# Top-k by a threshold and a counted mask in a windowed attention kernel

## What is computed

```python
k_windows = q_h[:, idx, :]                       # the 64 tokens up to this one
diff = k_windows - q_h[:, :, None, :]
dist = jnp.sqrt((diff * diff * m_h).sum(axis=-1) + 1e-08)
dist = jnp.where(mask[None], dist, jnp.inf)
neg_d, loc = jax.lax.top_k(-dist, K)             # K = 32 of 64
infl = jnp.exp(neg_d)
infl = infl / (infl.sum(axis=-1, keepdims=True) + 1e-08)
context = jnp.einsum('btk,btkd->btd', infl, neighbor_v)
```

## Time and profile before

| | |
|---|---|
| median of 3 runs | 865.25 us (864.89 to 867.82) |
| the profiled execution | 865.7 us |
| its span, first to last instruction | 863.9 us |
| mean granted TensorE clock | 0.895 of full speed |
| busy: DVE | 795.0 us, 92% of the span |
| busy: PE (matmuls) | 764.0 us, 88% |
| busy: ACT | 620.0 us, 72% |
| busy: POOL | 461.4 us, 53% |
| DMA | 27.27 MB in 49233 packets |

### The profile page before, as it was taken

One profiled execution on the slowest core, in us unless ns is written; L12 is line 12 of the kernel. 1 busy time (PEld: TensorE's weight loads), 2 busy tenths in 40 slices (PEclk: granted clock), 3 DMA queues, 4 the chain that ended last, 5 costly groups with the idle time before them and its releaser, 6 DMA issues.

```text
span 863.9 us, 21621 instructions
## 1 busy us (share of the span) xinstructions
PE 764.0 (88%) x4885; PEld 500.8 (58%) x4885; DVE 795.0 (92%) x6746; ACT 620.0 (72%) x1862; POOL 461.4 (53%) x870
## 2 busy tenths in 40 slices
PE   5987999998899999888989988999889898989975
PEld 3444556565566665556666655666556666655644
DVE  5865999799999998999999999979999999999890
ACT  3982466687777876777877787668777777877763
POOL 1113455565556665556666665556555565666442
PEclk9995777799999987999999999779999999998775
DMA  5300000010000000011001110001010100110000
GB/s 164 106 21 16 23 18 25 21 30 28 29 29 29 26 27 27 29 30 30 25 28 30 31 30 28 28 21 31 27 30 29 30 30 23 31 31 29 23 9 10
DMA packets 49233, 27.27 MB, mean 32 GB/s; under 512 B 5513, under 2 KB 48593, under 8 KB 49105
## 3 DMA queue, kind: packets, MB, share of 16 engines
q1 hardware_dynamic: 49104, 25.90, 10.1%
HBM read 10.28 MB, written 4.19 MB: 17 GB/s over the span
## 4 chain that ended last, share of the span: by engine, by line
DVE 75%; PE 17%; ACT 3%; issue 2%; DMA 2%; POOL 1%; SPq 0%; POOLq 0%; ACTq 0%
DVE work L939 39%; DVE m L929 26%; DVE key L955 4%; PE psC L1167 2%; PE psD L1112 2%; PE psW L1183 2%; PE psD L1012 2%; PE psD L1104 1%; DVE den L972 1%; DMA big<-in_x 1%; PE psW L1185 1%; PE psW L1194 1%; PE psW L1136 1%; PE psX L1119 1%; PE psC L1095 1%
## 5 line engine op out<-in xcount | busy, mean ns | idle before, releaser
L939 DVE MATCH_REPLACE8 work<-m,work 128x64 f32<-128x64 f32 x1536 | 300.6, 204 | 0.0
L929 DVE MAX8 m<-work 128x8 f32<-128x64 f32 x1536 | 210.2, 205 | 0.0
L471 POOL TENSOR_TENSOR big<-work,con 128x512 f32<-128x512 f32 x128 | 161.7, 1286 | 21.5 <-ACT work L617 21.5
L1167 PE MATMUL psC<-vst,big 128*128 128x34 f32 x1024 | 139.6, 282 | 0.0
L1167 PEld LDWEIGHTS psC<-vst,big 128*128 128x128 f32 x1024 | 125.2, 193 | 17.1 <-issue 2.1
L450 POOL TENSOR_TENSOR hsc<-gat,rnn 128x8 f32<-128x8 f32 x64 | 13.0, 204 | 222.4 <-ACT rnn L699 222.4
L1136 PE MATMUL psW<-con,big 128*128 128x128 f32 x512 | 92.2, 309 | 27.8 <-POOL big L471 19.5
L939 DVE MATCH_VALUE_LOAD work<-m,work 128x8 f32 x1536 | 113.0, 74 | 0.0
L1136 PEld LDWEIGHTS psW<-con,big 128*128 128x128 f32 x512 | 62.5, 155 | 64.7 <-POOL big L471 46.7
L939 DVE MATCH_REPLACE8 work<-m,key 128x64 f32<-128x64 f32 x512 | 99.9, 203 | 0.0
L676 ACT ACTIVATE key<-key,bias 128x512 f32<-128x512 f32 x64 | 46.2, 722 | 55.2 <-DVE key L955 55.2
(11 more groups left out here) (204 smaller groups left out, 1630.9 us busy)
## 6 DMA issues: line engine op xcount, KB each, us to landing
hst<-hT_all SPq DMA_DIRECT2D x64, 96.0 KB
tst<-qT_all SPq DMA_DIRECT2D x256, 17.0 KB
big<-in_x SPq DMA_DIRECT2D x16, 256.0 KB, 2.8
xs<-in_x SPq DMA_DIRECT2D x64, 64.0 KB, 1.9
out<-yo SPq DMA_DIRECT2D x64, 64.0 KB, 1.6
sst<-nst SPq DMA_DIRECT2D x128, 3.0 KB
tst<-nst SPq DMA_DIRECT2D x128, 2.0 KB
con<-in_consts SPq DMA_DIRECT2D x1, 549.5 KB, 5.4
```

What stands on the lines that cost most here:

```text
L471: nc.gpsimd.tensor_tensor(wun[:, s, heads].rearrange("p h (v j) -> p h v j", v=2), work[:, s].rearrange("p (h j) -> p h j", h=NH)[:, heads ...
L929: last = v.max(m8[:, h], src[:, h * WIN:(h + 1) * WIN])
L939: last = v.match_replace(work[:, s, cols], m8[:, h], src[:, cols], GONE)
L1167: last = mm(pC[:, h * 2 * VD:(h + 1) * 2 * VD], wts[:, s, h], vst[:, s4, h].rearrange("p v e -> p (v e)"), start=True, stop=True)
```

## The change

It alters what is selected, how, and the order of the queues.
- **Distances.** Each token half (64 rows) gets a matmul of its own with its own 160 columns (64 slots of the block before, 32 columns for query and low-rank product, 64 slots of its own block): 16 distance matmuls of 64 x 160 instead of 8 of 128 x 224. Masks shrink to 160 columns per group. Slot j of the result is a token by its place in the block, so key needs one relu (ACT) and one max/min (DVE).
- **Selection.** It runs on squared distances. Slots j and j+32 are compared: the smaller 32 go to one list, the negated larger 32 to the other. DVE takes the 16 largest of each list with two MAX8 rounds and one match_replace per head and list. The smallest of the 16 maxima of opposite ranks is the threshold theta, the value of the 32nd smallest.
- **Mask.** POOL subtracts theta from key (diff); PE transposes diff to slots in partitions; ACT takes Sign of diff + 1e-30 and of diff - 1e-30 (fst, bf16); two matmuls with count_bf count, so that of equal distances the right number is kept; DVE compares with KEEP and multiplies with the weight (wsel). The weights come from a transpose of key itself on PE (pXT), and Ln, Exp, Exp on ACT (infl).
- **Context.** POOL multiplies wsel by two 0/1 masks, of_own and of_before (wab). The slots already lie in partitions, so 8 matmuls (4 pairs of heads x 2) follow with values vst, which are kept per block of 64 tokens for a whole sequence. The 8 transposes and two copies to wts go, hst and its DMA go.
- **Order.** Output and second layer norm come a step later (chunk i-4). On ACT, infl of chunk i+1 and lnn, rnn stand ahead of yo of chunk i-4. On PE, the transpose of key of chunk i+1 stands behind the distances of chunk i+2. SP waits for yo of chunk i-4, then issues the copies for chunk i+3 as before, without hst. n_c moves from ACT to POOL.
- **Matmuls without a reader.** Three of 320 columns before the wait for wab, three of 256 before the wait for osp; the two of 240 columns ahead of the context and the two groups of 448-column ones go.

The diff, cut to its core:

```diff
-            def step(i, ph):
...
+            def step(i):
+                k = i - 4
+                if there(k):
                     sync.wait_ge(yo_ready, k + 1)
...
-                    sync.dma_start(hst[:, s], hT_all[:, bass.ds(c0, 3 * WIN)]).then_inc(rows_in[s], 16)
...
+                    sync.wait_ge(s_ready, k + 1)
                     for g in range(NG):
-                        sync.dma_start(sst[HD:P:32, s, g, 0:3 * WIN], nst[g:NH:NG, s]).then_inc(rows_in[s], 16)
+                        sync.dma_start(sst[HD:P:32, s, g].rearrange("p (n x) -> p n x", n=3)[:, :, 0:WIN],
+                                       nst[g:NH:NG, s].rearrange("p (n x) -> p n x", n=3)).then_inc(rows_in[s], 16)
...
+                    nc.gpsimd.tensor_tensor(diff.rearrange("p (h j) -> p h j", h=NH),
+                                            key[:, k % 2].rearrange("p (h j) -> p h j", h=NH),
+                                            theta[:, k % 2].unsqueeze(2).broadcast_to([P, NH, WIN]),
...
+                    nc.scalar.activation(fst[:, 0], pDT, ACT.Sign, bias=bias[:, 4:5]).then_inc(f_ready, 1)
+                    nc.scalar.activation(fst[:, 1], pDT, ACT.Sign, bias=bias[:, 5:6]).then_inc(f_ready, 1)
...
+                k = i + 1
+                if there(k):
+                    e = infl[:, k % 2]
...
+                    act.wait_ge(xT_ready, k + 1)
...
+                    nc.scalar.activation(e, pXT, ACT.Ln, bias=bias[:, 1:2]).then_inc(ln_done, 1)
...
+                    nc.scalar.activation(e, e, ACT.Exp, scale=0.5).then_inc(root_done, 1)
...
+                    nc.scalar.activation(e, e, ACT.Exp, scale=-1.0).then_inc(infl_ready, 1)
...
+                    nc.scalar.activation(lnn[:], n2[:, k % 4], ACT.Ln, bias=bias[:, 6:7]).then_inc(lnn_done, 1)
+                    act.wait_ge(lnn_done, k + 1)
+                    nc.scalar.activation(rnn[:, k % 2], lnn[:], ACT.Exp, scale=-0.5).then_inc(rnn_ready, 1)
+
+                k = i - 4
+                if there(k):
+                    act.wait_ge(y_ready, k + 1)
+                    need(act, po_ready, min(k + 3, NCH))
+                    need(act, out_in[k % 2], 16 * (k // 2))
...
+            def pick(rnd, u):
+
+                where = slice(8 * rnd, 8 * rnd + 8)
+                for h in range(NH):
+                    last = v.max(top[:, u, h, where], low_high[:, u, h])
+                last.then_inc(picked, 1)
+
+            def drop(u):
+
+                for h in range(NH):
+                    last = v.match_replace(low_high[:, u, h], top[:, u, h, 0:8], low_high[:, u, h], GONE)
...
+                    v.tensor_tensor(low_high[:, 1], x4[:, :, 0], x4[:, :, 1], ALU.max).then_inc(pair_done, 1)
+                    v.tensor_tensor(low_high[:, 0], x4[:, :, 0], x4[:, :, 1], ALU.min).then_inc(pair_done, 1)
+                    dve.wait_ge(pair_done, 3 * i + 1)
+                    v.tensor_scalar(low_high[:, 1], low_high[:, 1], -1.0, None, ALU.mult).then_inc(pair_done, 1)
...
+                    v.scalar_tensor_tensor(out=wsel, in0=pZ, scalar=KEEP, in1=infl[:, k % 2], op0=ALU.is_ge,
+                                           op1=ALU.mult).then_inc(w_ready, 1)
...
+                    v.scalar_tensor_tensor(out=meet, in0=top[:, 1], scalar=-1.0, in1=top[:, 0], op0=ALU.mult,
+                                           op1=ALU.max).then_inc(meet_done, 1)
+                    dve.wait_ge(meet_done, i + 1)
+                    need(dve, diff_ready, i - 1)
+                    v.tensor_reduce(theta[:, i % 2], meet, AX_X, ALU.min).then_inc(theta_ready, 1)
...
-                        last = mm(bank_of(r)[:, g, 0:SW], tst[strip, s, g], sst[strip, s, g], start=False,
-                                  stop=(g == NG - 1), skip_group_check=True)
+                        for late in range(2):
+                            toks = slice(late * WIN, (late + 1) * WIN)
+                            last = mm(bank_of(r)[toks, g, 0:PW], tst[strip, s, g, toks], sst[strip, s, g, late * B0:late * B0 + PW],
+                                      start=False, stop=(g == NG - 1), skip_group_check=True)
...
+                    keep_clock(psC, PW, 3)
+                    pe.wait_ge(wab_ready, 2 * k + 2)
...
+                        o = pC[:, r * 2 * VP:(r + 1) * 2 * VP].rearrange("p (v x) -> p v x", v=2)
+                        mm(o, wab[:, k % 2, 0, cols], vst[:, blk + 1:blk + 3, r], start=True, stop=False)
+                        last = mm(o, wab[:, k % 2, 1, cols], vst[:, blk:blk + 2, r], start=False, stop=True)
...
+                    mm(pZ, count_bf[:, 0], fst[:, 0], start=True, stop=False)
+                    mm(pZ, count_bf[:, 1], fst[:, 1], start=False, stop=True).then_inc(count_ready, 1)
...
+                k = i + 2
+                if there(k):
+                    pe.wait_ge(rows_in[k % 2], ROWS_IN * (k // 2) + ROWS_IN)
...
+                    distances(k % 2).then_inc(dist_ready, 1)
+
+                k = i + 3
+                if there(k):
...
+                k = i + 1
+                if there(k):
+                    pe.wait_ge(d2_ready, k + 1)
+                    need(pe, vst_ready, 2 * (k - 1))
+                    for r in range(4):
+                        last = nc.tensor.transpose(pXT[:, r * P:(r + 1) * P], key[:, k % 2, r * P:(r + 1) * P], ident)
+                    last.then_inc(xT_ready, 1)
...
+                    keep_clock(psX[:, 2 * P:4 * P], P, 3)
+                    pe.wait_ge(osp_ready, k + 1)
+                    nc.tensor.transpose(pO, osp[:, k % 2], ident).then_inc(po_ready, 1)
...
```

More of the change, by code:

```diff
@@ L54, in constants @@
     before = np.where(j > i, 0.0, BIG)
[L56 to L59, removed]
+    c[:, C_MASK:C_MASK + PW] = np.concatenate([before, np.zeros((P, QW)), own], 1)
+    slot = (np.arange(P) % WIN)[:, None]
+    tok = (np.arange(CH) % WIN)[None, :]
+    c[:, C_OWN:C_OWN + CH] = slot <= tok
+    c[:, C_OWN + CH:C_OWN + 2 * CH] = slot > tok
     e = np.arange(P) % 32
@@ L75, in constants, with counting, adaln_block @@
     return c
-def adaln_block(nc, x, encq, encv, w1, b1, w2, b2, base, hebu, hebv, dec, wr, amat, bmat, cin, wmod, consts, out):
+def counting():
+    jp, j = np.arange(WIN)[:, None], np.arange(WIN)[None, :]
+    eye, after = (jp == j).astype(np.float32), (jp >= j).astype(np.float32)
+    below, equal = 97.0 * eye - 1.0, 33.0 * eye - after
+    m = np.zeros((P, 2, P), np.float32)
+    for a in range(2):
+        rows = slice(a * WIN, (a + 1) * WIN)
+        m[rows, 0, rows] = 0.5 * (equal - below)
+        m[rows, 1, rows] = -0.5 * equal
+    return m
+def adaln_block(nc, x, encq, encv, w1, b1, w2, b2, base, hebu, hebv, dec, wr, amat, bmat, cin, wmod, consts, counts, out):
     ctx = ExitStack()
@@ L149, in adaln_block @@
         bsc = big[:].rearrange("p a s (b d) -> p (a s) b d", b=NB)
-        hst = sb("hst", [P, 2, 3 * WIN])
         tst = sb("tst", [P, 2, NG, CH])
         sst = sb("sst", [P, 2, NG, SW])
[L154 to L160, removed]
+        sqs = sb("sqs", [P, NG, 3 * WIN])
+        nst = sb("nst", [2 * NH, 2, 3 * WIN])
+        selm = sb("selm", [P, NB, NG, 2 * NH])
+        low_high = modn_all[:, 0:NH * WIN].rearrange("p (u h j) -> p u h j", u=2, h=NH)
+        top = gsgn_all[:].rearrange("p u (h n) -> p u h n", h=NH)
+        meet = gabs_all[:, 0].rearrange("p (h n) -> p h n", h=NH)
+        theta = sb("theta", [P, 2, NH])
+        diff = wmod_sb[:, 0:NH * WIN]
+        fst = sb("fst", [P, 2, 4 * CH], BF16)
+        infl = z8_all[:, 0:8 * CH].rearrange("p (s x) -> p s x", s=2)
+        wab = big[:, 0].rearrange("p s (v x) -> p s v x", v=2)
+        wsel = big[:, 1, 0, 0:4 * CH]
+        count_f = big[:, 1, 1, 0:2 * P]
+        vst = sb("vst", [P, NBLK, 4, VP])
         qh = sb("qh", [P, 4, NH, 2 * HD])
@@ new lines, in step @@
+                k = i - 1
+                if there(k):
+                    pool.wait_ge(w_ready, k + 1)
+                    need(pool, c_ready, k - 1)
+                    for v, part in enumerate((of_own, of_before)):
+                        nc.gpsimd.tensor_tensor(wab[:, k % 2, v].rearrange("p (r t) -> p r t", r=4),
+                                                wsel.rearrange("p (r t) -> p r t", r=4),
+                                                part.unsqueeze(1).broadcast_to([P, 4, CH]), ALU.mult).then_inc(wab_ready, 1)
@@ L506, in routing @@
                     pool.wait_ge(pG_ready, 2)
-            steps(pool, step, routing)
+            steps(step, routing)
         @block.scalar
@@ L727, in _ @@
+                k = i + 3
+                if there(k):
+                    act.wait_ge(pnn_ready, k + 1)
+                    need(act, gat_ready, k - 3)
+                    need(act, rnn_ready, k - 3)
+                    nc.scalar.activation(n2[:, k % 4], pNN, ACT.Copy, scale=-2.0).then_inc(n2_ready, 1)
+            steps(step, routing)
         @block.vector
@@ L1241 @@
         "consts": constants(),
+        "counts": counting(),
     }
```

697 lines of the change are left out of this document (353 added, 344 removed).

## The result

| | before | after |
|---|---|---|
| median of 4 runs each, us | 866.54 (864.89 to 871.47) | 980.98 (979.12 to 985.34) |
| profiled execution, its span, us | 865.7, 863.9 | 985.34, 983.6 |
| one step of the main loop, us (mean of 57) | 11.47 (11.72) | 13.68 (13.67) |

The ratio is 1.132, 95% interval 1.126 to 1.138: slower by 13%. The forecast was 960 us in a range of 885 to 1030. What stands behind it held in outline, with two terms of the sum, the distances and the clock, mis-sized in opposite directions.

The account below looks back on a forecast made before the run. DVE bounds the kernel before; afterwards a chain through SP should. Startup 90.5, 5 steps 58.5, 57 steps of 13.0 741, last two 21, tail 22: 933; plus clock 25 and 1.8 outside the span: 960 us, range 885 to 1030.

Parts of the forecast that it names:

- the distances: PE's 32 distance records of 160 columns in the chain: 1.5 us a step taken, between 0.7 and 2.1.
- the clock: Low TensorE clock stretches in the loop, each such step 5 us longer: 25 us in all (15 to 60).
- The chain and its order: ACT's yo, SP's copies, PE's masks to transposes, ACT's Ln: closes after one step, 13.0 us (12.1 to 14.3); chance 0.71.
- every sign asked of it: PE's masks wait each step, SP's idle ends with yo, 13 us steps, DVE below 75%, yo to masks 6.5 to 7.
- ACT's link: ACT's part of the chain, Ln, two Exp, lnn, rnn and yo: 2.8 us a step.
- SP and landing: SP's issue of output and row copies, 4.9 us, plus the last copy's landing, 1.75 us (1.6 to 2.4).
- the sum of the chain: ACT 2.8, SP 4.9, landing 1.75 and PE 3.6 us: 13.05 a step, taken as 13.0 after small overlaps.
- the small ones: DVE's work beside selection: d2 0.67, wsel alike, pair operations to theta 1.5, three waits near 0.1; DVE near 9.3 us.
- The five operations for which 1.5 us stood: On DVE, three 256-element pair operations, the meeting of the lists and the reduction to theta: 1 to 2 us together.
- Sign loads no table: Rival: on ACT, Sign needs another activation table, two loads a step, about 74 us on top, 1035; chance 0.03.
- The half-clock rival: Waits cost PE its clock, the loop is PE at half clock, half the steps 18 us: 1075 us; chance 0.09.
- The fast rival: Chain falls below 11.6 us, a path over ACT and PE decides at 10.8 to 11.1: 825 to 845 us; chance 0.13.

Follow-up runs that it names:

- the run with the clock held: Changed kernel with 16 readerless matmuls of 320 columns added ahead of PE's wait for the rows; 909.4 us, ratio 1.047 to the kernel before.
- the first experiment: Changed kernel with SP issuing the output copy, and its wait for yo, behind the row copies and xs; 866.51 us, ratio 0.996 to the kernel before.

## Why the prediction was right, point by point

- **The chain and its order: right.** It closes in one step, through the very queues named, and every sign asked of it is there: the wait at the masks in nearly every step (56 of them), yo as SP's releaser, 6.68 us from yo's end to the masks (6.5 to 7 foretold).
- **ACT's link: 2.61 us for 2.8.** Up to the next start Ln took 0.71 (0.76 foretold) and the last Exp 0.53 (0.63), since lnn starts before it ends. **SP and landing: 6.68 for 6.65.** The last needed issue starts near 512.16 and the masks start 1.6 us later, the lower end of the bounds and equal to the row of the output. The fixed 2.0 us of the Trainium skill, DMA: Bandwidth & Descriptors, "Anatomy of one DMA", would have been 0.4 too long; that section gives it for DMAs issued from GpSimd's queue, which the prediction didn't say, and these come from SP. The issue of the longer sst pattern takes 1.18 instead of 1.15 us, not up to 0.3 more.
- **Distances: the term was mis-sized.** At the full clock 32 records take 0.80 us, less than half of what the count of records gave as upper end, and less than the 1.04 of 16 wider ones. I took 1.5. That is 0.025 a record; the 0.065 of before, scaled to 160 columns, would be 0.046. So the two 64-row halves run beside each other. This is what the Trainium skill, TensorEngine Tiling (Array Packing), "Key Properties", states; the rule that I set against the row was the better one.
- **With that corrected the sum of the chain fits at the full clock.** 13.05 - 0.7 (distances) - 0.2 (ACT) = 12.15; the run with the clock held shows 12.11, and so do the few steps of the changed kernel itself that run at granted clock 1.00 throughout (187.71 to 199.82).
- **The clock: right sign, wrong place and size.** I had 25 us, as a few whole steps that grow longer than the chain. In fact most steps have their own slow stretch (of the 57 groups of masks seen behind the gap some 41 take over 1 us, the others 0.72, and in some of these the clock falls later, in pN), and it lies *inside* the chain, since the rows' gap stands directly ahead of masks, distances and pN. It costs 1.57 us in the step shown, 2.2 in those of 14.3 us, and 84 us in 57 steps, of which the run with the clock held gave back 72. This error and that of the distances nearly cancel: 57 x 13.67 = 779 us measured, 741 + 25 = 766 predicted. That the total came so close is therefore luck in part. The other 12.4 us of the difference in span (983.6 against 958.2) lie outside these steps; 3 of them ahead of the first MAX8 (93.48 for 90.49), of which the first pair operations and the negation, 91.34 to 93.48, are 2.1.
- **DVE: selection right, the small ones wrong.** 32 MAX8 take 3.2 us and 16 pairs 2.5, as worked out (3.2 and 2.6). But DVE is busy for 11.16 us a step, not 9.3, and 82% from 300 to 700 us, not below 75%. The five operations for which 1.5 us stood take 4.1 (1.29 + 0.29 + 0.98 + 1.26 + 0.28), because three wait beside POOL. Behind the chain that cost nothing, so the forecast didn't suffer. It decides what the change can bring without the chain. The Trainium skill, SBUF — State Buffer, "SBUF: two separate sides", describes this: a DVE operation with two SBUF inputs, or in a two-port mode, and a GpSimd operation that reads SBUF share a port pair as an exclusive lock, so the one that comes second blocks fully. The rows agree (0.29 becomes 1.25 to 1.32), the negation's too. I had not weighed it, though POOL's operations stood in the trace. ACT and PE were busy for less than I gave them: ACT for 7.0 us a step (8), PE for 8.6 in the step at the full clock (10).
- **Rivals.** Sign loads no table: two take 0.69 and 0.70 us, and the last ACT_TABLE_LOAD is at 63 us, ahead of the loop. The half-clock rival is false as stated: PE has gaps in every step and the mean clock is 0.831. The fast rival's 825 to 845 us is about where the kernel lands once the output is issued last and the clock held (842), but that is chance: the bound there is DVE, not the path over ACT and PE that this rival names.

So the loss comes from the output's place in SP's queue (all of the 114 us, by the first experiment), of which 72 come back if only the clock is held through the gap which that place opens. The saving on DVE went first behind the chain. With the chain cut, a part of it, 2.4 us a step, went into waits beside POOL.

## What to carry to other kernels

When a change reorders queues, look for a path that comes back to its own start one step later and sum it from rows; here the last copy of a finished result, issued ahead of the next inputs, made one. Charge a wait in front of PE not only with its length but with the clock of the work behind it, above all if that work is in the path. For each new DVE operation, ask which POOL operation runs beside it before taking its time from a row where it stood alone.

## What the runs showed of the hardware that was not expected

- The same gap of 2.3 us is followed by work at the low clock in most steps (3.7 us at granted clock 0.54 in the one shown), and in others by none: at 187.71 us the masks take 0.72 after a gap of 2.29, the next 3.69 us have granted clock 1.00, and the whole step takes 12.1 us. What decides between them isn't settled. Filled with readerless matmuls the gap never lowered it (1.00 from 300 to 700 us).
- Readerless matmuls can cost more than they save: without the six the version with the output last was 19 us faster, at nearly the same granted clock (0.85 for 0.88 from 300 to 700 us).
- Two kinds of work scale alike with the clock: pN 0.82 us at the full clock, 1.39 in the slow stretch; distances 0.80 and 1.37.
- DVE's operations of 128 and of 256 elements take the same 1.3 us when they begin together with a POOL instruction of 1.25 us.
